# Moving ScalarE's scaled copies between the exponentials of a selective scan

## The reference, cut to what matters

```
dt = softplus(ts @ W_dt.T + b_dt)          # (b, t, 2048)
A  = -exp(A_log)                           # (2048, 16)
for each token t:
    dA    = exp(dt_t[..., None] * A)       # (b, 2048, 16)
    state = state * dA + (dt_t * u_t)[..., None] * B_t[:, None, :]
    y     = einsum('bdn,bn->bd', state, C_t)
y = (y + x * D) * silu(gate);  out = y @ W_out.T
```

## Time and profile before

| | |
|---|---|
| median of three runs | 2945.51 us |
| profiled execution, its own time | 2944.21 us |
| its span in the trace | 2942.2 us |
| first to last exponential (L1179) | 159.1 to 2150.5 us |
| busy over the span: PE, DVE, POOL, ACT | 92%, 87%, 65%, 58% |

### The profile page before, as it was taken

How to read it: one execution, slowest core, us unless ns; L and a number is a source line. 1 busy time by engine, 2 the same in 40 slices (tenths; PEclk the granted TensorE clock), 3 DMA queues, 4 the chain that set the end, 5 groups by cost and what they waited for, 6 DMA issues and landing times.

```text
span 2942.2 us, 34577 instructions
## 1 busy us (share of the span) xinstructions
PE 2719.8 (92%) x10752; PEld 1515.4 (52%) x10752; DVE 2557.1 (87%) x3525; ACT 1695.6 (58%) x2852; POOL 1921.8 (65%) x886
## 2 busy tenths in 40 slices
PE   8998899999999999999999797888889999999996
PEld 3444555555555555555555454455544555555553
DVE  2388999999999999999999999999956787787785
ACT  2366556575665757556565654655525555555553
POOL 1178798898978989897898987989832222222221
PEclk9999999999999999999999998999999999999998
DMA  5442333443344344335333322322302111111110
GB/s 169 139 121 75 113 95 105 138 117 112 96 150 118 94 125 130 110 90 152 117 97 90 104 87 85 131 82 76 101 29 71 65 57 57 64 57 57 64 64 22
DMA packets 132873, 281.27 MB, mean 96 GB/s; under 512 B 12528, under 2 KB 12656, under 8 KB 132224
## 3 DMA queue, kind: packets, MB, share of 16 engines
q1 hardware_dynamic: 132736, 279.59, 31.4%
HBM read 245.86 MB, written 33.69 MB: 95 GB/s over the span
## 4 chain that ended last, share of the span: by engine, by line
PE 52%; DVE 32%; issue 10%; ACT 5%; POOL 2%; DMA 0%; DVEq 0%; POOLq 0%; SPq 0%; ACTq 0%
DVE arena L1443 16%; PE banks L533 14%; PE banks L557 9%; DVE arena L1459 7%; PE banks L634 7%; PE banks L773 4%; PE banks L726 4%; PE banks L682 3%; PE banks L707 3%; DVE arena L1389 2%; PE banks L697 2%; PE banks L737 2%; ACT banks L1179 1%; POOL arena L1357 1%; PE banks L569 1%
## 5 line engine op out<-in xcount | busy, mean ns | idle before, releaser
L1357 POOL TENSOR_TENSOR arena<-arena 128x2048 f32<-128x2048 f32 x255 | 1158.2, 4542 | 78.7 <-PE banks L634 78.7
L1443 DVE TENSOR_TENSOR_SCAN arena<-banks,arena 128x512 f32<-128x512 f32 x1024 | 1185.0, 1203 | 19.5 <-POOL arena L1357 13.5
L1179 ACT ACTIVATE banks<-arena,a_sb 128x508 f32<-128x508 f32 x1024 | 697.0, 684 | 700.4 <-DVE arena L1443 696.5
L533 PE MATMUL banks<-arena 128*128 128x512 f32 x2048 | 949.8, 601 | 11.7 <-DMA arena<-in_xT 8.4
L634 PEld LDWEIGHTS banks<-ident,arena 128*128 128x128 f32 x4096 | 489.2, 145 | 408.7 <-issue 170.6
L634 PE MATMUL banks<-ident,arena 128*128 128x128 f32 x4096 | 575.3, 284 | 122.0 <-DVE arena L1459 68.9
L533 PEld LDWEIGHTS banks<-arena 128*128 128x128 f32 x2048 | 373.8, 194 | 377.4 <-issue 373.1
L1459 DVE SCALAR_TENSOR_TENSOR arena<-banks,cg,arena 128x512 f32<-128x512 f32 x640 | 452.2, 737 | 42.5 <-PE banks L634 41.7
L557 PE MATMUL banks<-arena 128*128 128x512 f32 x1024 | 469.3, 597 | 5.4 <-DMA arena<-in_WoutT 4.1
L1370 POOL TENSOR_TENSOR arena<-arena 128x512 f32<-128x512 f32 x128 | 141.4, 1104 | 432.6 <-DVE arena L1624 432.5
L1289 POOL TENSOR_TENSOR arena<-arena 128x512 f32<-128x512 f32 x240 | 306.6, 1277 | 178.1 <-ACT arena L923 176.0
(11 more groups left out here) (142 smaller groups left out, 2937.4 us busy)
## 6 DMA issues: line engine op xcount, KB each, us to landing
arena<-b_scratch SPq DMA_DIRECT2D x128, 512.0 KB, 5.1
arena<-in_WinX SPq DMA_DIRECT2D x128, 256.0 KB, 2.9
arena<-in_WinZ SPq DMA_DIRECT2D x128, 256.0 KB, 2.8
arena<-in_WoutT SPq DMA_DIRECT2D x32, 1024.0 KB, 5.7
u_scratch<-arena SPq DMA_DIRECT2D x64, 256.0 KB, 5.0
arena<-u_scratch SPq DMA_DIRECT2D x16, 1024.0 KB, 9.4
arena<-x_scratch SPq DMA_DIRECT2D x32, 512.0 KB, 3.5
arena<-in_xT SPq DMA_DIRECT2D x14, 1024.0 KB, 8.2
```

Of the source, the lines that this page charges most:

```text
L533: last = nc.tensor.matmul(home(kind, i), wr[w % 2][:, k, :], x[:, k, :], start=(k == 0), stop=(k == KC - 1))
L1179: nc.scalar.activation(by_seq(bank(i % 2))[:, :, 1:SEQ], by_seq(dt[s % 2][:, i, :])[:, :, 1:SEQ], ACT.Exp, scale=a_sb[:, QD * q + i, n:n + ...
L1357: nc.gpsimd.tensor_tensor(hb[n % 4].rearrange("p (i t) -> p i t", i=QD), dtu, brep[pair % 3][:, n % 2:n % 2 + 1, :].broadcast_to([P, QD, G ...
L1443: nc.vector.tensor_tensor_scan(h, bank(i % 2), h, 0.0, ALU.mult, ALU.add)\
```

## The change

Before, ScalarE's copies stood behind all four exponentials of an index. Now, on a shared index, the copy of the third sequence stands behind the second exponential and that slot's other work, and the copy of the fourth behind the third exponential and that slot's other work. On a plain index the copy of the fourth sequence stands behind the second exponential and its slot's other work. No instruction is added or removed, and the order on TensorE, VectorE, GpSimd and the DMA queue is the same as before.

```diff
                     act_between(act, s, n, i)
-                if U >= 2:
-                    if (U - 2) % N in SHARED:
+                    if U >= 2 and i == 1 and (U - 2) % N in SHARED:
                         act_part2(act, (U - 2) // N, (U - 2) % N)
-                    act_part(act, (U - 2) // N, (U - 2) % N)
+                    if U >= 2 and i == (2 if (U - 2) % N in SHARED else 1):
+                        act_part(act, (U - 2) // N, (U - 2) % N)
```

## The result

The changed kernel takes 3000.32 us (median of three runs, 3000.19 to 3005.23) against 2945.51 us before. The ratio is 1.0192, with a 95% interval from 1.0178 to 1.0207: 1.9% slower. The prediction was 2995 us, with a range from 2952 to 3050.

The account below looks back on a forecast made before the run. VectorE was taken to bound the kernel. Late scans cost 39 us in steps 0 to 10 and 10 in steps 11 to 15, together 49 on 2944.21; forecast 2995 us, 1.7% slower, range 2952 to 3050.

Parts of the forecast that it names:

- What bounds the kernel: Inside the steps VectorE's own work, 98% busy, sets the pace; TensorE follows at 96%.
- The third exponential waits until 1.35 us after the transposes: With the copy ahead of the third exponential, the third scan can't start before 1.35 us after the transposes' end.
- The walk through step 6: Index by index through step 6, VectorE's and TensorE's lateness was summed; the step loses 3.55 us.
- 13 (GpSimd) and 15: Ahead of index 14, VectorE's 0.32 us wait for GpSimd was to be given back.
- the cover by the earlier slip: At indices 7 to 11, VectorE already over 1 us late against TensorE, so no copy stops it.
- my running sums: Two sums kept through step 6: how late VectorE is against before, and how late TensorE is.
- Carried to all steps: Step 6's 3.55 us taken for steps 0 to 10, 39 us; about 2.0 each for steps 11 to 15, 10 us.
- The rule that spoke against me: Skill's rule: take the highest-occupancy engine and shorten its gaps; by page averages TensorE, whose gap behind L937 the change shortens.
- A (TensorE's release wins): TensorE's released waits for L937, 34.2 us in all, make the kernel faster: 2922 us; chance 0.09.
- B (no cover): TensorE slips along, so every index pays for itself: 8 us a step, 129 us in all, 3074 us; chance 0.14.
- C: VectorE's delay vanishes in later slack and nothing changes: 2946 us; chance 0.07.

Follow-up runs that it names:

- mixed version: Kernel before with copies moved only where transposes end early enough (plain indices 4, 15; third sequence's copy on shared 0, 6, 12): 2945.22 us, ratio 1.000.
- the two halves: Against the kernel before, the change on the eleven plain indices alone, 2994.38 us, and on the five shared indices alone, 2975.60 us.

## Why the prediction was right

**What bounds the kernel.** Right. VectorE sets the pace. In step 6 of the mixed version the transposes of five indices came half a microsecond earlier and nothing was gained, while half a microsecond at an exponential shows in the step (index 6: 0.58).

**The third exponential waits until 1.35 us after the transposes.** Right in mechanism and size: 1.33 at index 5, and and, with everything one place earlier, 1.02 to 1.03 us for five plain indices of step 6 where the rule gives 1.0.

**The walk through step 6.** Right in its middle, off at both ends:

| index | forecast | measured |
|---|---|---|
| 0 | 0.20 | -0.53 |
| 3 | 0.48 | 0.61 |
| 5 | 1.07 | 1.11 |
| 6 | 0.58 | 0.58 |
| 9 and 12 | 0.54 | 0.65 |
| 14 | 1.0 | 0.53 |
| 13 (GpSimd) and 15 | -0.32 | -0.55 |
| step | 3.55 | 2.40 |

Indices 1, 2, 4, 7, 8, 10 and 11 kept their length to 0.01 us, as the cover by the earlier slip had said. At index 0 the transposes end 2.04 after the first scan instead of 2.71, and at index 14 2.12 instead of 2.67. TensorE had become 0.67 and 0.55 us earlier against VectorE than before, and my running sums had less of it.

**Carried to all steps: the step that failed.** "Steps 0 to 10 have the X tiles' sigmoids as slot work: 11 x 3.55 = 39" took them as one kind, and they are three. Steps 2, 4, 6, 8 and 10 cost 2.4 and not 3.55. Steps 5 and 9 cost 5.6 and steps 3 and 7 cost 6.8, with work that step 6 doesn't have: at index 2 the layer norm's shift (L1497) in steps 5, 9 and 13, and the reduction of the projections (L1408 and L1411) in steps 3, 7 and 11. In steps 5 and 9 the longer L1497 is 3.1 of the 3.2 us at index 2. In steps 3 and 7 three things add up. The first is one more late third and fourth exponential, 0.98 and 0.66 us in step 7:

```profile
1114.40 1.23 DVE L1443 TENSOR_TENSOR_SCAN arena<-banks,arena 128x512 f32<-128x512 f32 x1 [0.98 <-ACT banks L1179]
1116.29 1.22 DVE L1443 TENSOR_TENSOR_SCAN arena<-banks,arena 128x512 f32<-128x512 f32 x1 [0.66 <-ACT banks L1179]
```

My own rule would have found this from the trace of before. At index 2 of step 7 the transposes already ended at 1086.89, 2.84 us after the first scan, against 1.53 in step 6:

```profile
1084.05 2.33 DVE L1443 TENSOR_TENSOR_SCAN arena<-banks,arena 128x512 f32<-128x512 f32 x2
...
1085.85 1.04 PE L634 MATMUL banks<-ident,arena 128*128 128x128 f32 x8
```

The second is a small VectorE instruction that meets GpSimd's long multiply instead of a short one. The third is the clock.

For steps 11 to 15 I had said 10 us, and they cost 13.8. The mean granted clock fell there from 0.91 to 0.89, and no run tells how much of the loss that is. Too much in one kind of step and too little in the others nearly made up for each other: 49 us forecast and 55 measured. That the total came so close was in part luck.

**The rule that spoke against me.** By the page's averages TensorE comes first, at 92% in the changed kernel, and the edit took its wait for L937 away; the time rose by 1.9%. So the rule as I had put it, with the matmul row as TensorE's share, isn't borne out. I had used half of the section. The Trainium skill (Perfetto Trace Analysis, Identifying the Most-Contended Engine) also says to judge TensorE not by its matmul row but by its useful arithmetic against the peak and by the busy share of its weight loads. That share is 52% here, so VectorE, at 87%, comes first, and the runs agree with that.

**Rivals.** A (TensorE's release wins) fell with the mixed version. Its mechanism is half there: the release passes through, and it helps to keep index 7 on time in the changed kernel (0.97 us longer with the plain indices alone). B (no cover) fell with indices 7 to 11 of step 6 and with the two halves that cost 79 us apart and 55 together, but in steps 3 and 7 index 8 is late by 0.8 us, so the cover has gaps. C fell with the result.

## What to carry to other kernels

An in-order engine with a third of its time free can still set the pace, if an instruction that waits is put ahead of one that the bound engine needs. Before moving it, compare for each place the time at which its input arrives, plus what stands behind it, with the time at which the next consumer starts. Then do this for every kind of step and not for one, and look at which long instruction of a neighbour each small one will meet after the shift. A table of the change by index, from one profile each, shows where to keep a part of the edit: a few of its places made the kernel 0.23% faster, where all of them cost 1.9%.

## What the hardware showed that I had not expected

Two kinds of small VectorE instructions, L1411 and L1497, of 0.17 and 0.11 us when GpSimd was idle, lasted up to 4.38 us when they started while a GpSimd multiply of 4.5 us ran. They ended 0.02 to 0.03 us behind it each time, and the profile counts this as VectorE's busy time, so no list of waits shows it. VectorE's scans and sums, which read one operand from PSUM, ran beside the same multiplies at their usual 1.2 and 0.74 us, reductions of one operand in SBUF (L1408) at their 0.2 and 0.4 us, and memsets took 62 ns. The Trainium skill (SBUF — State Buffer, Who interferes with whom) has the rule: an SBUF port pair is shared between VectorE and GpSimd and held exclusively for a whole instruction, and a VectorE instruction with two SBUF inputs, or in a two-port mode, blocks behind a GpSimd one. By this rule, L1497 (two SBUF inputs) and, in a two-port mode, L1411 are such instructions. The trace agrees in when they end, to 0.03 us; no run here shows which mode L1411 was in.

In steps 3 and 7 of the changed kernel, a wait of TensorE for VectorE (2.23 us in step 7) was followed by some 3.4 us at a granted clock of 0.50. That made the next transposes late, and VectorE waited 1.20 us for them. Before, the same place in step 7 had a wait of 2.17 us and the full clock. The stretch costs 1.3 us at index 4 of step 7. Which of two such waits the clock falls behind can't be told from the wait itself in these traces, and small moves of time made such stretches come and go in steps 5, 7, 8 and 9.
